# Four state-space and patch layers on one core: B rows copied ahead of the first tile's side work, and four slots for the blocks of the convolution layer

## The chip, the cores and the metric

The kernel runs on 1 core of one Trainium2 chip. The metric is the device time of one execution in microseconds. In the text PE is TensorE, ACT is ScalarE, DVE is VectorE, POOL is GpSimd and SP is SyncE, which only issues DMAs here.

## The reference, cut to what matters

x has the shape (4, 32, 32, 96): 4 images of L = 1024 positions and 96 channels. Four layers are added to it one after the other, each on the group norm of x.

```python
x = x + L0(_gn(x))    # selective scan, 4 directions, 192 channels, 16 states
x = x + L1(_gn(x))    # patches and their nearest neighbour ("motif")
x = x + L2(_gn(x))    # 3x3 convolution, then a selective scan in 1 direction
x = x + L3(_gn(x))    # as L0
```

The heart of L0, L2 and L3 is the scan over the 1024 positions, for each channel d and state n:

```python
dt = softplus(dt_proj(...) + bias)             # delta
h  = exp(dt * A[d, n]) * h + dt * u * B[n]     # along the positions
y  = sum_n h * C[n]  +  u * D
```

Behind it stand a layer norm over the channels, a product with silu(z) and an output projection.

## The kernel before

**Tiles.** A tile is 128 partitions x 1024 positions: 64 channels (a block, c = 0, 1, 2 of 192 channels) times two states. A group is the three tiles of one pair of states, which share a B row and a C row; each row is spread over 64 partitions by DMA. In L0 and L3 a turn is one image in one of two orders of its positions (row-wise, column-wise) with both directions: 2 directions x 8 pairs of states x 3 blocks = 48 tiles, t = 0 to 47, in 16 groups. There are 8 turns for each of these layers; turns 0, 2, 4 and 6 are the even ones (`r = 0`), and turns 2, 4 and 6 also finish the image before. L2 has 4 turns of 24 tiles, one for each image.

**What each tile costs.** ACT makes the decay exp(delta * A) into one of three buffers (L732, in L2 L1343). DVE makes the product of du and the B row (L872, in L2 L1480) in PSUM and then scans decay and product into one of three state buffers (L887, L1502). POOL multiplies the state by the C row into one of two read buffers (L796, L1394), and PE adds that into the y banks (L609, L1192). All of them work in program order and wait on counting semaphores.

**The B row.** `b_rows` holds one row tile. `copy_b` (L722, L1314) takes it to PSUM, where two buffers alternate by group and the spare one also holds the products of tiles c = 0 and 1. It waits for its DMA and for the scan of tile c = 1 of the group before:

```python
act.wait_ge(b_in, 32 * (G + 1))
act.wait_ge(scanned, (G - 1) * NBLK + 2 + SCAN0)
nc.scalar.copy(b_ps[g % 2][:, :], b_rows[:, :]).then_inc(b_ready, 1)
```

DVE waits for `b_ready` before the product of a group's tile c = 0. The copy stands in ACT's program ahead of decay(c=1), behind decay(c=0) and all that ACT does after that. A decay waits for the scan three tiles earlier, so decay(c=1) and the copy of a group wait for the same scan.

**Sides.** Between the tiles the engines do other work: u, bc, dt and sum of the softplus for the next turn, z, shift, cent, var and out for the image that was finished. A table gives each side product (`("dt", 2): (36, 37)` and so on, in halves) a place in PE's order of tiles, plus or minus a lag: PE computes it at tile `at` into the single PSUM bank `side_ps`, ACT takes it at tile `at + 4` (DVE cent, shift and out at `at + 3`). The next side product waits on PE until the bank is free, and the y matmuls of the tile stand behind it. The softplus has steps exp, log, one, less and relu on ACT (`ACT_SOFTPLUS`), gap and du on POOL (`POOL_SOFTPLUS`). In an even turn, ACT has at tile 36 dt2's first half and exp 1, at 37 its second half and log 1, at 38 sum 0 and one 1, at 39 sum 0's second half, less 1 and exp 2; POOL has gap 1 after read 36, and du 0 after read 37.

**SP's queue.** For each group g it issues the b row of g + 1 (`load_b`, L493, waits for copy g), then its c row (`load_c`, L504, waits for the reads of group g - 1). In L0 and L3 it also copies the blocks of delta and du of the next turn into `delta2` and `du2`, which hold every block on both halves of the partitions (L477, L478, at g = 13 and 14 of even turns, 11 and 12 of odd ones). In L2 `delta2` and `du2` have three slots, one for each block, and SP copies all three after the turn's last group, behind the c and b rows of the next turn: the copies of block q wait until the last decay and the last product of block q are done.

Of the kernel before, what the change touches and what calls it, by code (L numbers as in the profile page):

```python
# [11 lines left out]
L = H * W  # L12
# [324 lines left out]
def cross_scan_layer(nc, name, x_cm, g_cm, ident, cols_e, hbm, rank, eps):  # L337
# [4 lines left out]
    with cleared(nc) as (ctx, sems):  # L342
# [286 lines left out]
        def _(act):  # L629
# [93 lines left out]

            def turn_of(turn):
                o, number = turn.r, turn.number
                for t, (d, p, c) in enumerate(tiles):
# [198 lines left out]
def conv_scan_layer(nc, name, x_cm, g_cm, ident, hbm, rank, eps):  # L925

    NT, NJ = CONV_TILES, 2
# [5 lines left out]
    with cleared(nc) as (ctx, sems):  # L933
# [67 lines left out]
        delta2 = sb("delta2", [128, NBLK, L])  # L1001
        du2 = sb("du2", [128, NBLK, L])
# [31 lines left out]

        block = ctx.enter_context(nc.Block())
# [5 lines left out]
        def _(sp):  # L1041
# [4 lines left out]
            def copy_rows(dst, src, q, done):  # L1046

                for side in range(2):
                    if q < 2:
                        sp.dma_start(dst[quarter(side), q, :], src[0][quarter(q), :]).then_inc(done, 16)  # L1050
                    else:
                        for i, s in halves():
                            sp.dma_start(dst[quarter(side), q, s], src[1][quarter(i), :]).then_inc(done, 16)
# [42 lines left out]
            for turn in turns:  # L1096
                for g in range(NP):
# [111 lines left out]
        def _(act):  # L1209
# [120 lines left out]

            for _, key, i in head.sides:
# [3 lines left out]
            for turn in turns:  # L1335
                number = turn.number
                for t, (p, c) in enumerate(tiles):
# [5 lines left out]
                    nc.scalar.activation(decay[:, t % DECAYS, :], delta2[:, c, :], ACT.Exp,  # L1343
                                         scale=a_neg[:, c, p:p + 1]).then_inc(decay_ready, 1)
                    for at, key, i in turn.sides:
# [284 lines left out]
```

## Time and profile before

| what | value |
|---|---|
| median of 3 runs | 3991.15 us (3986.45 to 3998.62) |
| the profiled execution | 3994.56 us, its span 3992.8 us |
| granted TensorE clock, mean | 0.749 |
| PE busy | 2839.3 us, 71% |
| DVE busy | 3267.8 us, 82% |
| ACT busy | 2053.4 us, 51% |
| POOL busy | 2350.5 us, 59% |
| scans of L0 and L3 (L887) | 768, 2286 ns each |
| products of L0 and L3 (L872) | 768, 1221 ns each |
| copies of a B row (L722) | 256, 1016 ns each |

The profile is one execution. L0's turns run from 125 to 1535 us of its span, L1 until about 1760, L2's turns from 1869 to 2325, and L3's from 2505 to 3912. Times of an instruction in the rows are from the start of the span. The granted clock is that of TensorE, 1.0 being 2.4 GHz.

### The profile page before, as it was taken

To read this page: it belongs to the slowest core of one execution; us is meant where nothing else is said; L and a number is where in the kernel's file an instruction comes from. 1 tells how busy PE (TensorE), PEld (TensorE's weight loads), DVE (VectorE), ACT (ScalarE), POOL (GpSimd) and SP (SyncE) were. 2 spreads that over 40 slices of the span, in tenths; PEclk is the share of its full clock that TensorE was granted. 3 is DMA by queue.
4 is the path that set the end of the run, shared out by engine and by line. 5 is a ranking of instruction groups with operands and counts; after the bars stand their busy time and mean duration, and the time that the engine had idled before them with its cause. 6 is when DMAs were issued, how large, how long until landed. Compare 5 with 4: busy or idle time off the path is not lost. (4 is left out here: it accounts for less than half of the span.)

```text
span 3992.8 us, 26321 instructions
## 1 busy us (share of the span) xinstructions
PE 2839.3 (71%) x5888; PEld 626.3 (16%) x5888; DVE 3267.8 (82%) x2104; ACT 2053.4 (51%) x2278; POOL 2350.5 (59%) x1004
## 2 busy tenths in 40 slices
PE   3678878877877787105576664678778877887886
PEld 1111111111111111001111111111111111111111
DVE  1799999999999994373888730899999999999992
ACT  2465555656565562113455423466555656656561
POOL 0577767767676773001655521677767767776772
PEclk9767788788778775556798765677787788778885
DMA  1655556554655652002424401555636555554651
GB/s 37 138 126 133 135 124 148 130 137 113 143 133 131 142 122 54 16 4 67 105 67 105 113 14 41 135 126 132 156 102 158 129 130 122 137 135 119 156 131 32
DMA packets 140329, 436.92 MB, mean 109 GB/s; under 512 B 33383, under 2 KB 34093, under 8 KB 139869
## 3 DMA queue, kind: packets, MB, share of 16 engines
q1 hardware_dynamic: 140188, 435.53, 45.5%
q14 instruction: 112, 0.92, 0.1%
q8 instruction: 29, 0.48, 0.1%
HBM read 307.50 MB, written 6.82 MB: 79 GB/s over the span
## 5 line engine op out<-in xcount | busy, mean ns | idle before, releaser
L796 POOL TENSOR_TENSOR L_read<-L_state,L_c_rows 128x1024 f32<-128x1024 f32 x768 | 1809.4, 2363 | 754.3 <-DVE L_state L887 469.3
L887 DVE TENSOR_TENSOR_SCAN L_state<-L_decay,L_b_ps 128x1024 f32<-128x1024 f32 x768 | 1756.0, 2286 | 29.0 <-DVE L_b_ps L872 2.1
L609 PE MATMUL L_y_ps<-L_read,L_fold 128*64 128x512 f32 x3072 | 1251.0, 910 | 398.5 <-POOL L_read L796 378.3
L872 DVE TENSOR_TENSOR L_b_ps<-L_du,L_b_ps 128x1024 f32<-128x1024 f32 x768 | 937.6, 1221 | 261.6 <-issue 173.8
L732 ACT ACTIVATE L_decay<-L_delta,L_a_neg 128x1024 f32<-128x1024 f32 x768 | 876.7, 1146 | 411.2 <-DVE L_state L887 410.3
L722 ACT COPY L_b_ps<-L_b_rows 128x1024 f32<-128x1024 f32 x256 | 260.1, 1016 | 340.1 <-DVE L_state L887 217.6
L609 PEld LDWEIGHTS L_y_ps<-L_read,L_fold 128*64 128x64 f32 x3072 | 187.6, 161 | 1360.7 <-POOL L_read L796 1005.6
L1394 POOL TENSOR_TENSOR L_read<-L_state,L_c_rows 128x1024 f32<-128x1024 f32 x96 | 237.2, 2474 | 199.6 <-PE L_y_ps L1192 101.0
L589 PE MATMUL L_side_ps<-g_cm,L_w_u 96*128 (+1 forms) x216 | 189.0, 966 | 85.3 <-ACT L_u L650 45.4
L589 PE MATMUL L_side_ps<-L_dbl,L_w_dt 128*128 128x512 f32 x216 | 195.2, 1002 | 60.9 <-DVE L_sq_b L858 26.9
L1502 DVE TENSOR_TENSOR_SCAN L_state<-L_decay,L_b_ps 128x1024 f32<-128x1024 f32 x96 | 219.5, 2286 | 3.3
L1480 DVE TENSOR_TENSOR L_b_ps<-L_du,L_b_ps 128x1024 f32<-128x1024 f32 x96 | 117.3, 1222 | 95.1 <-DMA L_du<-L_du_a 75.4
L661 ACT COPY L_delta<-L_side_ps 128x512 f32<-128x512 f32 x108 | 63.1, 584 | 230.3 <-PE L_side_ps L589 230.3
L1192 PE MATMUL L_y_ps<-L_read,L_fold 128*64 128x512 f32 x384 | 125.8, 733 | 66.7 <-POOL L_read L1394 54.0
L1343 ACT ACTIVATE L_decay<-L_delta,L_a_neg 128x1024 f32<-128x1024 f32 x96 | 109.2, 1144 | 109.0 <-DMA L_delta<-L_delta_a 49.4
L1372 POOL TENSOR_TENSOR L_l_a<-L_more,L_l_a 128x1024 f32<-128x1024 f32 x4 | 9.4, 2350 | 238.1 <-ACT L_more L1272 238.1
L774 POOL TENSOR_TENSOR L_y_b<-L_more,L_y_b 128x1024 f32<-128x1024 f32 x18 | 42.6, 2365 | 168.9 <-ACT L_more L692 168.9
L589 PE MATMUL L_side_ps<-L_delta,ident 128*128 128x512 f32 x216 | 124.7, 662 | 0.0
L780 POOL TENSOR_TENSOR L_du<-L_delta,L_u 128x1024 f32<-128x1024 f32 x36 | 85.4, 2372 | 26.4 <-ACT L_delta L661 26.4
L786 POOL TENSOR_TENSOR x_cm<-x_cm,L_sq_b 96x1024 f32 (+1 forms) x8 | 18.8, 2354 | 137.2 <-DVE L_sq_b L858 137.2
L162 PE MATMUL motif_ps<-ident,motif_acc 128*96 128x128 f32 x32 | 6.4, 396 | 121.3 <-DVE motif_acc L272 121.3
L650 ACT COPY L_u<-L_side_ps 128x512 f32<-128x512 f32 x108 | 61.9, 573 | 53.9 <-PE L_side_ps L589 53.4
(301 smaller groups left out, 2718.2 us busy)
## 6 DMA issues: line engine op xcount, KB each, us to landing
L_c_rows<-L_bc_dram SPq DMA_DIRECT2D x580, 256.0 KB, 4.0
L_b_rows<-L_bc_dram SPq DMA_DIRECT2D x580, 256.0 KB, 4.1
L_delta<-L_delta SPq DMA_DIRECT2D x204, 256.0 KB, 5.6
L_du<-L_du SPq DMA_DIRECT2D x140, 256.0 KB, 5.7
L_du<-L_u SPq DMA_DIRECT2D x64, 256.0 KB, 6.0
L_bc_dram<-L_dbl SPq DMA_DIRECT2D x40, 128.0 KB, 3.4
L_delta<-L_delta_a SPq DMA_DIRECT2D x16, 256.0 KB, 6.6
L_du<-L_du_a SPq DMA_DIRECT2D x16, 256.0 KB, 7.0
```

Source lines behind the costliest of these rows:

```text
L589: m = nc.tensor.matmul(side_ps[0:rows, :], lhs, rhs, start=(k == 0), stop=(k == len(parts) - 1))
L609: m = nc.tensor.matmul(y_ps[i * BLK:(i + 1) * BLK, c, :], fold[:, :], y_half(t, o, i), start=first, stop=last, skip_group_check=True)
L722: nc.scalar.copy(b_ps[g % 2][:, :], b_rows[:, :]).then_inc(b_ready, 1)
L732: nc.scalar.activation(decay[:, t % DECAYS, :], delta2[:, d * NBLK + c, :], ACT.Exp, scale=a_neg[:, o * 2 + d, c, p:p + 1]).then_inc(decay ...
L796: nc.gpsimd.tensor_tensor(read[:, t % READS, :], state[:, t % STATES, :], c_rows[:, g % 2, :], ALU.mult).then_inc(multiplied, 1)
L872: nc.vector.tensor_tensor(to[:, :], du2[:, d * NBLK + c, :], row[:, :], ALU.mult).then_inc(injected, 1)
L887: nc.vector.tensor_tensor_scan(state[:, t % STATES, way], decay[:, t % DECAYS, way], fed[:, way], 0.0, ALU.mult, ALU.add).then_inc(scanned, 1)
L1192: m = nc.tensor.matmul(y_ps[quarter(i), c, :], fold[:, :], read[:, t % READS, s], start=t < NBLK, stop=t >= NT - NBLK, skip_group_check=True)
L1343: nc.scalar.activation(decay[:, t % DECAYS, :], delta2[:, c, :], ACT.Exp, scale=a_neg[:, c, p:p + 1]).then_inc(decay_ready, 1)
L1394: nc.gpsimd.tensor_tensor(read[:, t % READS, :], state[:, t % STATES, :], c_rows[:, p % 2, :], ALU.mult).then_inc(multiplied, 1)
L1480: nc.vector.tensor_tensor(to[:, :], du2[:, c, :], row[:, :], ALU.mult).then_inc(injected, 1)
L1502: nc.vector.tensor_tensor_scan(state[:, t % STATES, :], decay[:, t % DECAYS, :], fed[:, :], 0.0, ALU.mult, ALU.add).then_inc(scanned, 1)
```

## The change

In the three scan layers ACT's side work moves into a function `side_work(turn, t)`. It is no longer called after decay(c=0). After decay(c=1) it is called for both tiles, c = 0 and c = 1, and after decay(c=2) for that tile. The copy of a group's B row, still ahead of decay(c=1), is thereby ahead of the side work of tile c = 0. `take_y` (at tile 3) keeps its place. In L2 `delta2` and `du2` get four slots instead of three, and block q of an image lies in slot (3 * image + q) mod 4. A copy waits for the block that had the slot four blocks earlier. The copies of block 0 for the next image are issued at g = 6, after the b and c rows of the last group and ahead of the rows for the next image; blocks 1 and 2 stay at the end of the turn.

The diff, without the part that repeats it for L2's ACT program and the slot index in reads and writes:

```diff
@@ cross_scan_layer, block.scalar @@
+            def side_work(turn, t):
+
+                for at, key, i in turn.sides:
+                    if at == t - ACT_LAG and key[0] in ACT_SIDES:
+                        take(turn, key, i)
+                if turn.finish and t == SILU_AT:
+                    silu(turn)
+                if turn.finish and t == RSTD_AT:
+                    root(turn)
+                for (kind, j), at in ACT_SOFTPLUS[turn.r].items():
+                    if at == t:
+                        softplus(turn, kind, j)
+
             def turn_of(turn):
                 o, number = turn.r, turn.number
                 for t, (d, p, c) in enumerate(tiles):
...
-                    for at, key, i in turn.sides:
-                        if at == t - ACT_LAG and key[0] in ACT_SIDES:
-                            take(turn, key, i)
                     if turn.finish and t == Y_AT:
                         take_y(turn.done_image)
-                    if turn.finish and t == SILU_AT:
-                        silu(turn)
-                    if turn.finish and t == RSTD_AT:
-                        root(turn)
-                    for (kind, j), at in ACT_SOFTPLUS[o].items():
-                        if at == t:
-                            softplus(turn, kind, j)
+                    for since in ((), (t - 1, t), (t,))[c]:
+                        side_work(turn, since)
@@ conv_scan_layer @@
-    NT, NJ = CONV_TILES, 2
+    NT, NJ, SLOTS = CONV_TILES, 2, NBLK + 1
...
-        delta2 = sb("delta2", [128, NBLK, L])
-        du2 = sb("du2", [128, NBLK, L])
+        delta2 = sb("delta2", [128, SLOTS, L])
+        du2 = sb("du2", [128, SLOTS, L])
...
+        def slot(image, q):
+            return (image * NBLK + q) % SLOTS
...
             def copy_block(image, q):
 
                 sp.wait_ge(sp_du, image * NJ + q // 2 + 1)
-                if image > 0:
-                    sp.wait_ge(decay_ready, (image - 1) * NT + NT - NBLK + q + 1)
-                copy_rows(delta2, delta, q, delta2_in[q])
-                if image > 0:
-                    sp.wait_ge(injected, (image - 1) * NT + NT - NBLK + q + 1 + INJECT0)
-                copy_rows(du2, du, q, du2_in[q])
+                was, last = divmod(image * NBLK + q - SLOTS, NBLK)
+                if was >= 0:
+                    sp.wait_ge(decay_ready, was * NT + NT - NBLK + last + 1)
+                copy_rows(delta2, delta, image, q, delta2_in[q])
+                if was >= 0:
+                    sp.wait_ge(injected, was * NT + NT - NBLK + last + 1 + INJECT0)
+                copy_rows(du2, du, image, q, du2_in[q])
...
                     if g == CONV_STORE and turn.next is not None:
                         store_bc(turn)
+                    if g == NP - 2 and turn.next is not None:
+                        copy_block(turn.next, 0)
                 if turn.next is not None:
-                    for q in range(NBLK):
+                    for q in range(1, NBLK):
                         copy_block(turn.next, q)
```

## Rows read from the trace of the kernel before

**Rows 1.** the page, part 1: busy us (share of the span) xinstructions, by engine
```profile
PE 2839.3 (71%) x5888; PEld 626.3 (16%) x5888; DVE 3267.8 (82%) x2104; ACT 2053.4 (51%) x2278; POOL 2350.5 (59%) x1004
```

**Rows 2.** waits: engine, line, <- whom, us in total, times, longest
```profile
DVE L_b_ps L1480 <- DMA L_du<-L_du_a: 75.4, 8, 53.4
DVE L_b_ps L872 <- ACT L_b_ps L722: 67.3, 42, 4.6
```

**Rows 3.** timeline, DVE, L0 turn 4 (start, us, instruction, [idle <-releaser]): tiles 39, 45
```profile
973.45 1.23 DVE L872 TENSOR_TENSOR L_b_ps<-L_du,L_b_ps 128x1024 f32<-128x1024 f32 x1 [1.04 <-ACT L_b_ps L722]
...
998.83 1.23 DVE L872 TENSOR_TENSOR L_b_ps<-L_du,L_b_ps 128x1024 f32<-128x1024 f32 x1 [4.18 <-ACT L_b_ps L722]
```

**Rows 4.** timeline, ScalarE, the same turn: copy 12 to copy 15
```profile
958.39 1.02 ACT L722 COPY L_b_ps<-L_b_rows 128x1024 f32<-128x1024 f32 x1 [0.34 <-DVE L_state L887]
959.34 1.14 ACT L732 ACTIVATE L_decay<-L_delta,L_a_neg 128x1024 f32<-128x1024 f32 x1
...
966.06 0.59 ACT L661 COPY L_delta<-L_side_ps 128x512 f32<-128x512 f32 x1 [2.44 <-PE L_side_ps L589]
...
970.32 1.15 ACT L692 ACTIVATE L_more<-L_more,L_minus_col 128x1024 f32<-128x1024 f32 x1
...
997.69 1.02 ACT L722 COPY L_b_ps<-L_b_rows 128x1024 f32<-128x1024 f32 x1 [4.81 <-DMA L_b_rows<-L_bc_dram]
```

**Rows 5.** timeline, PE, the same turn: dt2's second half, sum's first
```profile
957.16 1.13 PE L589 MATMUL L_side_ps<-L_dbl,L_w_dt 128*128 128x512 f32 x2 [1.13 <-ACT L_delta L659]
...
961.69 2.07 PE L589 MATMUL L_side_ps<-L_y_a,ident 128*128 128x512 f32 x2 [2.39 <-ACT L_delta L659]
```

**Rows 6.** timeline, GpSimd, the same turn: the gap of block 1
```profile
971.61 2.36 POOL L774 TENSOR_TENSOR L_sq_b<-L_more,L_sq_b 128x1024 f32<-128x1024 f32 x1 [2.06 <-ACT L_more L692]
```

**Rows 7.** timeline, SyncE's queue, the same turn
```profile
980.96 1.08 SPq L504 DMA_DIRECT2D L_c_rows<-L_bc_dram  x2
...
990.85 2.35 SPq L493 DMA_DIRECT2D L_b_rows<-L_bc_dram  x2
```

**Rows 8.** timelines, ScalarE and DVE, L3 turn 6: less, tile 45
```profile
3699.77 1.15 ACT L692 ACTIVATE L_more<-L_more,L_minus_col 128x1024 f32<-128x1024 f32 x1
...
3728.28 1.23 DVE L872 TENSOR_TENSOR L_b_ps<-L_du,L_b_ps 128x1024 f32<-128x1024 f32 x1 [3.70 <-ACT L_b_ps L722]
```

**Rows 9.** timeline, all engines, L0 turn 4, tile 15
```profile
877.88 0.59 ACT L652 COPY L_dbl<-L_side_ps 128x512 f32<-128x512 f32 x1 [0.24 <-PE L_side_ps L589]
...
878.78 1.10 PE L589 MATMUL L_side_ps<-L_gate_a,L_w_ob_a 128*96 128x512 f32 x2
...
880.07 1.02 ACT L722 COPY L_b_ps<-L_b_rows 128x1024 f32<-128x1024 f32 x1 [1.60 <-DVE L_state L887]
...
883.40 0.66 DVE L855 TENSOR_TENSOR x_cm<-x_cm,L_side_ps 96x512 f32 x1
```

**Rows 10.** timelines, SyncE's queue and DVE, L0 turn 5, tile 39
```profile
1140.86 2.13 SPq L493 DMA_DIRECT2D L_b_rows<-L_bc_dram  x2
...
1148.66 1.23 DVE L872 TENSOR_TENSOR L_b_ps<-L_du,L_b_ps 128x1024 f32<-128x1024 f32 x1
```

**Rows 11.** timelines, L2 turn 1: PE and DVE at tile 15, DVE at tiles 21, 22
```profile
2054.04 1.07 PE L1177 MATMUL L_side_ps<-L_gate_a,L_w_ob_a 128*96 128x512 f32 x2 [1.05 <-ACT L_delta_b L1240]
...
2056.44 0.72 DVE L1462 SCALAR_TENSOR_TENSOR x_cm<-L_side_ps,L_out_bias,x_cm 96x512 f32<-96x512 f32 x1
...
2088.55 1.23 DVE L1480 TENSOR_TENSOR L_b_ps<-L_du,L_b_ps 128x1024 f32<-128x1024 f32 x1 [5.76 <-ACT L_b_ps L1314]
...
2093.10 0.68 DVE L1466 TENSOR_TENSOR L_sq_b<-L_sq_a,L_side_ps 96x512 f32<-96x512 f32 x1 [1.00 <-PE L_side_ps L1177]
```

**Rows 12.** timelines, L2, end of turn 1: GpSimd, SyncE's queue, DVE
```profile
2083.68 2.34 POOL L1377 TENSOR_TENSOR L_du_a<-L_delta_a,L_u_a 128x1024 f32<-128x1024 f32 x1
...
2096.48 1.18 SPq L1050 DMA_DIRECT2D L_delta<-L_delta_a  x2
...
2106.09 1.23 DVE L1480 TENSOR_TENSOR L_b_ps<-L_du,L_b_ps 128x1024 f32<-128x1024 f32 x1 [4.81 <-DMA L_du<-L_du_a]
```

More of the change, by code:

```diff
@@ L1044, in _, with copy_rows @@
                 sp.dma_start(to, src).then_inc(weights, 16)
-            def copy_rows(dst, src, q, done):
+            def copy_rows(dst, src, image, q, done):
                 for side in range(2):
                     if q < 2:
-                        sp.dma_start(dst[quarter(side), q, :], src[0][quarter(q), :]).then_inc(done, 16)
+                        sp.dma_start(dst[quarter(side), slot(image, q), :], src[0][quarter(q), :]).then_inc(done, 16)
                     else:
                         for i, s in halves():
-                            sp.dma_start(dst[quarter(side), q, s], src[1][quarter(i), :]).then_inc(done, 16)
+                            sp.dma_start(dst[quarter(side), slot(image, q), s], src[1][quarter(i), :]).then_inc(done, 16)
             def copy_block(image, q):
                 sp.wait_ge(sp_du, image * NJ + q // 2 + 1)
-                if image > 0:
-                    sp.wait_ge(decay_ready, (image - 1) * NT + NT - NBLK + q + 1)
-                copy_rows(delta2, delta, q, delta2_in[q])
-                if image > 0:
-                    sp.wait_ge(injected, (image - 1) * NT + NT - NBLK + q + 1 + INJECT0)
-                copy_rows(du2, du, q, du2_in[q])
+                was, last = divmod(image * NBLK + q - SLOTS, NBLK)
[5 more added lines that the diff above has]
+                copy_rows(du2, du, image, q, du2_in[q])
             def store_bc(stage):
@@ L1329, in after, with side_work @@
                     root(stage)
+            def side_work(turn, t):
+                for at, key, i in turn.sides:
+                    if at == t - ACT_LAG and key[0] in CONV_ACT_SIDES:
+                        take(turn, key, i)
+                if t == CONV_SILU_AT:
+                    silu(turn)
+                if t == CONV_RSTD_AT and turn.done is not None:
+                    root(turn)
+                if turn.next is not None:
+                    for kind, j in CONV_ACT.get(t, ()):
+                        softplus(turn, kind, j)
             for _, key, i in head.sides:
@@ L1342, in _ @@
                     act.wait_ge(scanned, number * NT + t - DECAYS + 1 + SCAN0)
-                    nc.scalar.activation(decay[:, t % DECAYS, :], delta2[:, c, :], ACT.Exp,
+                    nc.scalar.activation(decay[:, t % DECAYS, :], delta2[:, slot(number, c), :], ACT.Exp,
                                          scale=a_neg[:, c, p:p + 1]).then_inc(decay_ready, 1)
-                    for at, key, i in turn.sides:
-                        if at == t - ACT_LAG and key[0] in CONV_ACT_SIDES:
-                            take(turn, key, i)
                     if t == CONV_Y_AT and turn.done is not None:
                         take_y(turn.done)
-                    if t == CONV_SILU_AT:
-                        silu(turn)
-                    if t == CONV_RSTD_AT and turn.done is not None:
-                        root(turn)
-                    if turn.next is not None:
-                        for kind, j in CONV_ACT.get(t, ()):
-                            softplus(turn, kind, j)
+                    for since in ((), (t - 1, t), (t,))[c]:
+                        side_work(turn, since)
             take_y(B - 1)
@@ L1479, in inject_tile @@
                     dve.wait_ge(scanned, T + SCAN0)
-                nc.vector.tensor_tensor(to[:, :], du2[:, c, :], row[:, :], ALU.mult).then_inc(injected, 1)
+                nc.vector.tensor_tensor(to[:, :], du2[:, slot(number, c), :], row[:, :], ALU.mult).then_inc(injected, 1)
                 return to
```

## The prediction

> **What bounds the kernel now.** I read the page first: DVE is busy 82% of the span, more than any engine [rows 1]; in a scan layer that is one product (L872) and one scan (L887) for each tile, about 3.6 us together. What can be won is its idle time between tiles, so the second view was its waits [rows 2]: 67.3 us in 42 waits for the copy of the B row (L722) in L0 and L3, and in L2 75.4 us for the DMAs of du, 53.4 of them before the first image. The 173.8 us of "issue" are the heads of two layers, which the change leaves alone. The third view was the timeline of each engine around every such wait, since only it tells what the copy itself was waiting for.
>
> It shows two kinds. In 7 waits at tile 39 of an even turn (1.04 us in the one of [rows 3]) the copy stands behind side work of tile 39. In the eight at tile 45 (4.18 us in [rows 3], some 34 us of the 67 in all) it waits for its row: the copy comes 4.81 us after ScalarE went idle, released by a DMA [rows 4]. In 14 more, at tile 0 (0.5 to 1.7 us), it again waits for the row. A place in ScalarE's queue can't mend a late row.
>
> **Part 1: the order on ScalarE.** Instructions and durations stay (768 decays, 256 copies, the same sides). Side work of a group's first tile (c = 0) used to follow decay(c=0). Now it follows copy and decay(c=1). Both of these wait for the scan of two tiles back, one tile later than decay(c=0) had to. So this work comes up to one tile (3.6 us) plus copy plus decay (0.95 + 1.05 us from start to start, [rows 4]) later, with ScalarE idle meanwhile. Behind it stand PE's next side matmuls (one PSUM bank, freed by ScalarE) and the y matmuls behind them, GpSimd's products, SyncE's transfers. Nothing else fills the hole: before L661 at 966.06 ScalarE idles 2.44 us with later work queued [rows 4]. The Trainium skill, page PSUM — Partial Sum Buffer, section Engine vs sequencer instructions, calls ScalarE's queue strict first in, first out, which speaks against this change; by that rule, the trace agrees, held side work costs what is worked out below, and were the queue free to reorder, the part would be the pure gain of the first rival.
>
> *Even turns, tiles 36 to 45 (8 of them).* Turn 4 of L0. Before the change dt2's first half and its exp run ahead of the copy at 958.39 and free the bank for PE at 957.16 [rows 4, 5]. After the change: decay 36, idle, copy 958.4, decay 37 at 959.3, and dt2 at 960.4; the bank is free at 961.6. PE's next dt2 matmuls go from 957.16 to 961.7, ScalarE takes them at 962.8 to 964.0, PE's "sum" starts at 964.1 instead of 961.69. It now takes 4.4 us (to L661 at 966.06), its second half 2.9; so it is taken at 967.0 to 968.5. After that come "one" (1.0), decay 39 (1.1), copy 13 (1.0), decay 40 (1.1), "sum" (0.5), and "less" starts at 972.0 to 973.5, not 970.32: 1.7 to 3.2 late. I take 3.0, since PE has stood idle for some 5 us before, where after 2.39 us [rows 5] its matmuls already took twice as long. Copy 13 is at 969.5 to 971.0: the stall at tile 39 is gone.
> What does "less" release? GpSimd's gap, at 971.61 after 2.06 us of waiting [rows 6]. From there GpSimd has no pause (gap, read 37, du, read 38: four of 2.36 us) until read 38 releases the c rows at 980.96; behind them SyncE issues eight copies until 990.85, then the b row of tile 45 [rows 7], which is copied at 997.69. Tile 45 thus starts "less" + 28.5 us, whatever DVE does. L3's turn 6 bears this out: DVE has no stall at tile 39 there, and still tile 45 starts 28.51 us behind "less" (3699.77 to 3728.28, [rows 8]), to the hundredth as here (970.32 to 998.83). So 1.04 us won at tile 39 buys nothing, and 3.0 us lost at "less" arrive whole: **8 x 3.0 = +24** (13 to 26; to 37 if both sums run at the lower clock, 1.5 us more each).
>
> *Tile 15 of turns that finish an image (6 in L0 and L3).* "bc" of tile 15 is taken at 877.88, PE's shift runs from 878.78, and DVE adds it at 883.40 without waiting: 2.6 us spare [rows 9]. New: copy 880.07, decay 881.02, bc 882.1 to 882.7, shift from 882.8 to 884.8, so DVE waits 1.4 us; queued up from earlier (silu of tile 10 now starts 2.6 us late) 0.4 more. I take 1.8; at the lower clock the shift takes 3.9 and it is 3.5. **6 x 1.8 = +11** (9 to 21).
>
> *Odd turns (8).* u2 and "less" of tile 30, sum of tile 33 and sum and less of tile 36 come 2 to 4 us late. Read 32 releases c rows and eight copies, behind which the b row of tile 39 is issued at 1140.86, and DVE starts that tile at 1148.66 without a wait [rows 10]. This chain moves 1.5 to 2.7 us, against a spare of some 0.6 there and 1.3 at the next tile 0. In the four turns with stalls at 33 and 36 those go, and are mostly found again at 39. **8 x 0.7 = +6** (-4 to +12).
>
> *L2.* At tile 21 of turns 1 and 2 the copy lies behind "sum" and "var" and DVE waits 5.76 us. It will no longer. But the next thing on DVE, the out product, starts at 2093.10, released by PE at the end of the chain var, root, out [rows 11], which doesn't move: 2 x 5.76 us are only shifted 5 us on. **0** (-1 to 0). Tile 15 has the same shift as above: PE's shift starts at 2054.04, released by dt1's L1240, and DVE takes it at 2056.44 at once [rows 11]; with copy and decay first PE starts at 2056.5 and DVE at 2058.6, +2.1, and a similar 0.3 at tile 18. Turn 3 gets some 1.8 in all. **2 x 2.4 + 1.8 = +7** (0 to 12).
>
> **Part 2: four slots in L2.** At each of three image changes DVE waits for du at tiles 0 and 1: 75.4 - 53.4 = 22.0 us [rows 2], 1.3 of them in the first image. The copies can't start now before the last scans release the slots and stand behind one another on SyncE: delta from 2096.48, two issues of 1.18 us in all, then du and block 1 [rows 12]; DVE starts at 2106.09 after 4.81 us [rows 12]. With a fourth slot block 0 moves ahead of the c and b rows, right behind GpSimd's du (2083.68 + 2.34, [rows 12]), 10 us earlier, and needs no wait for a slot; its wait on SyncE holds up nothing, as the c rows behind it wait for a read until 2094. Blocks 1 and 2 take the times that blocks 0 and 1 had (four issues, 3.5 us), so block 1 lands at 2106.0, needed at 2104.9, and block 2 about when needed. Left are about 1 us there, some 3 in turn 1 for the b row (its issue comes behind the c rows and it takes about 4 to land), and 0.5 to 1 more for the copy of tile 3, which stays behind take_y. That is 5.1 each: **-15.4** (-8 to -21, nearly all of it). [...]
>
> **Sum.** +24 + 11 + 6 + 0 + 7 - 15.4 = +32.6. The profiled execution took 3994.6 us (span 3992.8), 3.4 over the median 3991.15; changes carry over, so 3991.15 + 32.6 = **4024 us**.
>
> **Rivals.**
> 1. *The waits on the copy were the loss, as counted* (PE and GpSimd absorb the later sides). Gone: 67.3 less 34 (tile 45) and 15 (tile 0) = 18, 11.5 at tile 21, 15.4: -45, 3946 us. For it: the waits name the copy [rows 3]. Against: the 28.51 us that hold with and without a stall at tile 39 [rows 3, 8], and out in L2. It decides if "less" starts no later than now. 10%.
> 2. *Only the slots count*: the sides come late but within spare time everywhere (the tile-15 slack of 2.6 us suffices, sum runs at full clock behind an early dt2). -15, 3976 us. 12%.
> 3. *The lower clock joins in*: idle PE falls to 1.2 GHz and both sums and the shift take the long time: 37 + 21 + 12 + 9 - 12 = +67, 4058 us. 10%.
> Forecast, with its own range 4000 to 4045: 68%.
>
> A measurement here tells 0.3% (12 us) from no change. Slower, above 4003: 64 of the forecast's 68 and rival 3, 74%. Same: its other 4 and 6 of rival 2, whose 3976 lies near the bound, 10%. Faster: rival 1 and the rest of rival 2, 16%. The range leaves out rival 1, a third of rival 2 and half of rival 3, 19%: 3970 to 4057.
>
> **What would show it.** DVE's waits on L722 lose those at tiles 33, 36 and 39 of the old places, but those at 45 grow from 4.3 to 8 or are partly turned into waits for GpSimd (scan 41 needs read 38, now at 984); new waits of the shift add (L855 in L0 and L3, L1462 in L2) for PE, 1.5 to 3.5 us; in L2 5.8 us more before L1466; du waits at image changes down from 21 to 2 to 7. Wrong would be: "less" of an even turn at its old place, no waits at L855, or tile 45 early although "less" is late.

## The result, and the profile after

| | before | after |
|---|---|---|
| median of 6 runs beside each other | 3990.68 us (3981.49 to 3998.62) | 4065.03 us (4062.0 to 4082.8) |
| span of the profiled execution | 3992.8 us | 4061.4 us |
| granted TensorE clock, mean | 0.749 | 0.735 |

The ratio is 1.0194, with an interval of 1.0172 to 1.0217: 74 us slower, where the prediction had 33 and a range that ended at 4057. The direction was right and the size was not.

The page of after, part 1, and its list of DVE's waits (us in total, times, longest), which answer to [rows 1] and [rows 2]:

```profile
PE 2868.5 (71%) x5888; PEld 635.9 (16%) x5888; DVE 3264.4 (80%) x2104; ACT 2045.5 (50%) x2278; POOL 2345.3 (58%) x1004
```

```profile
DVE x_cm L860 <- PE L_side_ps L589: 79.9, 10, 24.4
DVE L_b_ps L877 <- ACT L_b_ps L722: 76.2, 36, 5.2
DVE L_b_ps L1496 <- DMA L_du<-L_du_a: 54.7, 2, 53.4
DVE x_cm L1478 <- PE L_side_ps L1188: 45.4, 7, 20.9
...
DVE L_state L892 <- POOL L_read L801: 41.9, 35, 2.6
```

The reader is to see that no engine has more work: the instructions are as many as before, DVE's busy time is 3 us less and its share falls from 82 to 80%. Only PE is busy longer, 29 us, with the same 5888 matmuls at a lower mean clock. The waits grew. Those on the copy are 76.2 us, not 67.3, so the change makes longer what it was to remove. The shift add (L860, L855 before) waits 79.9 us in 10 places, 57.7 us in 5 before. The scans wait 41.9 us for GpSimd's reads, 0.8 before. Only du's DMAs in L2 went down, from 75.4 to 54.7 us.

The starts of the products in the timelines of both kernels give the length of each stretch of a turn, and so the place of the loss. Sums over all such turns, us, after against before:

| stretch | predicted | measured |
|---|---|---|
| finishing turns, tiles 0 to 15 (6) | +11 | +23.4 |
| even turns, tile 33 to the end (8) | +24 | +26.7 |
| odd turns (8) | +6 | +21.8 |
| L2, up to L3's first product | -8.4 | -0.3 |
| the rest (-3.9 of it ahead of L0's first product) | 0 | -3.0 |
| sum | +32.6 | +68.6 |

The term of the even turns is near what was reckoned, those of tile 15 and of the odd turns are far too small, and what L2 was to win did not come. The sum is that of the two profiled executions; the medians are 74.4 us apart.

These lengths scatter from one execution to another. In `slots_only`, `order_l2`, `held_6`, `held_9_15`, `held_15` and `held_15_fill` below, the even turns behind tile 33 and the odd turns are those of before, and yet their sums differ from before's by -9.9 to +2.1 us (even) and by -4.4 to +2.7 (odd). Before's own trace is thus on the long side in even turns: against the other traces the change costs some 31 us there, the mean, and not 26.7.

### The profile page after: what moved, and what is told of

It is laid out like the page before. It is cut to its first block and busy times, and to the rows that moved or that the text cites. A ratio compares the mean times of both kernels' runs of the same rounds, so it can differ in the third digit from the quotient of the medians.

```text
span 4061.4 us, 26320 instructions
## 1 busy us (share of the span) xinstructions
PE 2868.5 (71%) x5888; PEld 635.9 (16%) x5888; DVE 3264.4 (80%) x2104; ACT 2045.5 (50%) x2278; POOL 2345.3 (58%) x1004
## 5 line engine op out<-in xcount | busy, mean ns | idle before, releaser
L892 DVE TENSOR_TENSOR_SCAN L_state<-L_decay,L_b_ps 128x1024 f32<-128x1024 f32 x768 | 1755.8, 2286 | 69.3 <-POOL L_read L801 41.9
L609 PE MATMUL L_y_ps<-L_read,L_fold 128*64 128x512 f32 x3072 | 1268.0, 925 | 361.6 <-POOL L_read L801 343.2
L1496 DVE TENSOR_TENSOR L_b_ps<-L_du,L_b_ps 128x1024 f32<-128x1024 f32 x96 | 117.3, 1222 | 71.5 <-DMA L_du<-L_du_a 54.7
L1203 PE MATMUL L_y_ps<-L_read,L_fold 128*64 128x512 f32 x384 | 131.5, 765 | 52.5 <-POOL L_read L1410 45.4
L589 PE MATMUL L_side_ps<-L_delta,ident 128*128 128x512 f32 x216 | 116.3, 621 | 0.0
L589 PEld LDWEIGHTS L_side_ps<-L_dbl,L_w_dt 128*128 128x128 f32 x216 | 47.9, 276 | 287.6 <-ACT L_delta L659 165.5
```

The costliest lines, as they stand in the source:

```text
L589: m = nc.tensor.matmul(side_ps[0:rows, :], lhs, rhs, start=(k == 0), stop=(k == len(parts) - 1))
L609: m = nc.tensor.matmul(y_ps[i * BLK:(i + 1) * BLK, c, :], fold[:, :], y_half(t, o, i), start=first, stop=last, skip_group_check=True)
L892: nc.vector.tensor_tensor_scan(state[:, t % STATES, way], decay[:, t % DECAYS, way], fed[:, way], 0.0, ALU.mult, ALU.add).then_inc(scanned, 1)
L1203: m = nc.tensor.matmul(y_ps[quarter(i), c, :], fold[:, :], read[:, t % READS, s], start=t < NBLK, stop=t >= NT - NBLK, skip_group_check=True)
L1496: nc.vector.tensor_tensor(to[:, :], du2[:, slot(number, c), :], row[:, :], ALU.mult).then_inc(injected, 1)
```

## Experiments

All are the kernel before with parts of the change, unless it says otherwise. Times stand against the runs of before made beside them.

**The change in its parts.** `slots_only` has part 2 alone, `order_l2` and `order_l0` have the new order on ScalarE in L2 alone or in L0 and L3 alone. The edits are those of the diff above, layer by layer. `copy_only` moves the copy in L0 and L3 ahead of the side work, but leaves decay(c=1) behind it:

```diff
                     if c == 1:
                         copy_b(number * GROUPS + p + NP * d, (p + NP * d))
+                        side_work(turn, t - 1)
...
-                    for since in ((), (t - 1, t), (t,))[c]:
-                        side_work(turn, since)
+                    if c > 0:
+                        side_work(turn, t)
```

> Before with part 2 alone: four slots in L2, block 0 copied at g = 6, ScalarE's old order in all layers. The traces of before and after show L2 as a whole at -0.3 us. Theory: the slots win what was reckoned for them, and the new order in L2 gives it back: -8 to -15 us, so 3976 to 3983, and the product's waits for du (L1480 in before) fall from 22 to under 7 us outside the first image. Rival: the waits for du only turn into waits for the B row and the copy at the same place, and nothing is won: 3988 to 3994.

> Before with the new order on ScalarE in L2 alone, three slots. Theory (the counterpart of the one for the slots): +7 to +15 us, 3998 to 4006, from new waits of the shift add at tile 15 and 18 (4 us each in the trace of after) and from the out product. Rival: L2's order change is neutral, the stall of 5.76 us at tile 21 pays for the two shift waits: 3988 to 3994.

> Before with the new order in L0 and L3 alone, nothing changed in L2. From the lengths of the turns in the two traces: finishing turns up to tile 33 +24, even turns behind it +27, odd turns +22, heads -4, together +69: 4055 to 4065. Rival: the slots or L2 have a share in the loss (through the granted clock, which fell from 0.749 to 0.735): 4030 to 4050.

> Before with the copy alone moved, in L0 and L3: decay(c=0), copy, side work of tile c = 0, decay(c=1), side work of c = 1. The copy waits for the same scan as decay(c=1), so the side work is still held for it, but by a decay (1.05 us) less, and the side work of two tiles is parted by a decay. Theory: the wait for the scan in front of the side work is what costs; 60 to 90% of the loss of the kernel with the new order in L0 and L3, +42 to +62, 4033 to 4053. Rival: it is the decay put in front and the two tiles' work in one piece that cost, as two halves of a side product must pass one bank: under a third of the loss, 3991 to 4013.

| kernel | median, us | against before | ratio, interval |
|---|---|---|---|
| slots_only | 3970.03 | -19.9 | 0.9954 (0.9940 to 0.9967) |
| order_l2 | 4006.62 | +16.7 | 1.0040 (1.0026 to 1.0054) |
| order_l0 | 4066.78 | +76.8 | 1.0190 (1.0173 to 1.0207) |
| copy_only | 4027.63 | +37.7 | 1.0093 (1.0077 to 1.0108) |

The three parts add up to +73.6, and the whole change has +74.4, so each can be judged by itself. The order in L0 and L3 is most of the miss (+76.8 where 24 + 11 + 6 = 41 was reckoned, 36 of the 42 us). The slots give somewhat more than I expected here, and in L2 the order costs more than the 7 of the prediction. `copy_only` came out at half of `order_l0`, below my 60 to 90% and above the rival's third, so both matter: that side work waits for the copy's scan, and that decay(c=1) stands ahead of it as well. By stretches, the copy alone costs 1.8 us up to tile 15 of the finishing turns, where the whole order costs 23.1, then 11.9 for 29.7 in even turns and 14.4 for 20.6 in odd ones.

**Which group holds what.** In the next kernels the new order holds for single groups of tiles only. `held_6` has group 2 of the finishing turns, `held_9_15` their groups 3 to 5, `held_15` group 5. `held_a`, `held_b` and `held_c` have one group in each of three stretches. The edit of `held_b`, set against the new order:

```diff
-                    for since in ((), (t - 1, t), (t,))[c]:
+                    late = t // NBLK in (10,) if o else t // NBLK in (4, 12,)
+                    for since in (((), (t - 1, t), (t,))[c] if late else (t,)):
                         side_work(turn, since)
```

> Before, with the new order on ScalarE in the six finishing turns of L0 and L3 for group 2 alone (tiles 6 to 8), old order everywhere else. The kernel with the new order throughout L0 and L3 loses 23.1 us between tiles 0 and 15 of these turns. In the windows, PE is busy 13.7 to 14.1 of 14.1 us in tiles 4 to 7 of before, at a clock of 0.95 to 0.98. Theory: this is the stage with no slack; z's halves held at tile 6 make a backlog on PE that reaches the shift at tile 15, six times 2 to 4: +12 to +23, 4002 to 4013, with new waits of the shift add (L860 here) at tile 15. Rival, the prediction's own account: only what is held at tile 15 counts, and a hold at tile 6 is made good before it: 3987 to 3994.

> Before, with the new order in the six finishing turns for groups 3 to 5 alone (tiles 9 to 17: u, silu, bc). The prediction's account: 6 x 1.8 = +11 (9 to 21), 3999 to 4012. Theory of the backlog from tiles 4 to 8: here the turn gets to tile 9 without one, so the wait at tile 15 is 0.5 to 1.8 us, +3 to +11, 3993 to 4001; the two together leave the 23.1 us of the whole to both.

> Before with the new order on ScalarE in L0 and L3 for single groups only: group 3 (tiles 9 to 11: u0, silu) and group 11 of even turns, group 9 (tiles 27 to 29) of odd ones. Read by stretches of a turn. The prediction's account: 0.4 us at most at tile 15, nothing in odd turns, even turns nothing at tile 33. Rival (a hold works through groups before): 1 us or more at tile 15, 1 us or more in odd turns between tiles 27 and 39.

> The same for group 4 (tiles 12 to 14: u1, bc) and group 12 of even turns (tiles 36 to 38: dt2, exp, sum), group 10 of odd ones (tiles 30 to 32: u2, less, sum). The prediction's account: nothing at tile 15, most of the 3.0 us behind tile 39 in even turns, under 1 us in odd turns. Rival: 1 to 3 us at tile 15 through u1, and 2 to 3 us in odd turns, as less at tile 30 holds GpSimd's gap and with it all reads up to the c row.

> The same for group 5 (tiles 15 to 17: bc) and group 13 of even turns (tiles 39 to 41: sum, less, exp), group 11 of odd ones (tiles 33 to 35). The prediction's account: 1.4 us at tile 15, some 1 us behind tile 39 in even turns (less behind decay 40), -1.4 in those odd turns that have a stall at tile 33. Rival: nothing at tile 15 when the groups before it are on time (2.6 us spare), the loss of 3.7 us there needs groups 3 to 5 together.

`held_6` took 3986.55 us, ratio 0.9993 (0.9983 to 1.0003): nothing. My theory of the backlog from tile 6 fell, and the prediction's account held there. `held_9_15` took 4011.47 us, +22.4, ratio 1.0060 (1.0046 to 1.0075). Growth by stretches in the traces (sums over the turns, us; the last three kernels ran once each, at 3992.96, 4054.53 and 4028.99 us):

| kernel | finishing, 0 to 15 | even, 33 to end | odd, whole |
|---|---|---|---|
| order_l0 | +23.1 | +29.7 | +20.6 |
| held_9_15 | +20.1 | | |
| held_a (groups 3; 11; 9) | +3.6 | -7.8 | +2.8 |
| held_b (groups 4; 12; 10) | +17.5 | +20.0 | +20.5 |
| held_c (groups 5; 13; 11) | +17.4 | +10.8 | +3.7 |

In even turns groups 12 and 13 together make 30.8, the whole order 29.7, in the proportion that the prediction gave them; with the scatter above, this sum can be off by several us. In odd turns group 10 alone makes all of it. Up to tile 15, group 4 alone or group 5 alone costs nearly as much as groups 3 to 5 together (group 5 some 3.3 us in five turns, group 4 1 us in two turns and 3.2 to 5.2 in four). The four are just those in which the granted clock was 0.53 to 0.54 in tiles 4 to 7, ahead of the held group; in the other two it was 0.98 and 0.75. What group 4 costs by itself is thus the 1 us, and the rest goes with the clock. The -7.8 of `held_a` lies within the scatter. "less" of tile 39 has two places there, 19.1 to 20.5 us or 17.6 us behind the start of tile 33. The later one came in seven even turns of before and in two of `held_a`. What decides between them is not shown.

ScalarE's timeline shows the hold of group 10, in turn 5 of L0 of `held_b`:

```profile
1126.69 1.15 ACT L745 ACTIVATE L_decay<-L_delta,L_a_neg 128x1024 f32<-128x1024 f32 x1 [0.85 <-DVE L_state L893]
1130.27 1.02 ACT L722 COPY L_b_ps<-L_b_rows 128x1024 f32<-128x1024 f32 x1 [2.43 <-DVE L_state L893]
1131.22 1.15 ACT L745 ACTIVATE L_decay<-L_delta,L_a_neg 128x1024 f32<-128x1024 f32 x1
1132.27 0.56 ACT L650 COPY L_u<-L_side_ps 128x512 f32<-128x512 f32 x1
```

and the same place of before, whose turn began at 1010.52, not at 1027.43:

```profile
1109.79 1.15 ACT L732 ACTIVATE L_decay<-L_delta,L_a_neg 128x1024 f32<-128x1024 f32 x1 [0.85 <-DVE L_state L887]
1110.84 0.57 ACT L650 COPY L_u<-L_side_ps 128x512 f32<-128x512 f32 x1
...
1113.37 1.02 ACT L722 COPY L_b_ps<-L_b_rows 128x1024 f32<-128x1024 f32 x1 [0.91 <-DVE L_state L887]
```

u2's first half is taken 104.84 us after the turn's start, 100.32 before: 4.5 us later, and 2.43 of them ScalarE stands idle with this work ready. It is the full price of a hold: the wait for the scan, the copy (0.95) and the decay (1.05). SyncE's issue of tile 39's row, 130.34 us after the turn's start before [rows 10], comes at 134.53 here:

```profile
1161.96 2.16 SPq L493 DMA_DIRECT2D L_b_rows<-L_bc_dram  x2
```

So 4.2 of the 4.5 us come through, not 1.5 to 2.7.

**The shift at tile 15.** One question was left here. With group 5 held, bc's second half is taken 51.8 us after the turn's start, as the prediction had it (882.1 less 830.3). Still DVE waits 3.2 us, not 1.4. `held_15` has group 5 of the finishing turns alone, and `held_15_fill` adds two matmuls with weights of zero in the hole on PE, so PE idles less ahead of the shift (the lines that set up `zero_w` are left out):

```diff
+                    if turn.finish and t == 12:
+                        for _ in range(2):
+                            nc.tensor.matmul(y_ps[0:BLK, 0, :], zero_w[0:C, :], g_half(turn.next_image, 0, 0),
+                                             start=False, stop=False, skip_group_check=True)
                     for at, key, i in turn.sides:
                         if at == t:
                             side(turn, key, i)
```

> Before with the new order on ScalarE in L0 and L3 for group 5 alone (tiles 15 to 17) of the finishing turns. In the kernel that also had other groups in other stretches, tiles 0 to 15 of these turns grew by 3.4 us each (one 1.0), and PE stood idle for 2.0 us ahead of the shift. Expected: the same here, 17 to 23 us in all, 4003 to 4012.

> The same, and on PE two matmuls of the shift's length with weights of zero ahead of the shift's first half in these turns (they add zero to y), in the 2 us in which PE otherwise waits for bc. Theory: it is the lower granted clock after the idle time that makes the shift take 4.1 us instead of 2.0; with the hole filled the shift runs at 2.4 GHz and the wait at tile 15 falls from 3.4 to 1.0 to 1.8 us: 10 to 14 us under the kernel without the filling. Rival: the clock has nothing to do with it, or the filling itself stands in the way: the wait stays at 3.4 us or grows, same time or slower.

Timeline of PE at the shift of tile 15, L0 turn 4, and under it what the shift add waited (DVE), `held_15`:

```profile
883.57 1.88 PE L589 MATMUL L_side_ps<-L_gate_a,L_w_ob_a 128*96 128x512 f32 x2 [3.81 <-ACT L_dbl L652]
885.38 2.02 PE L589 MATMUL L_side_ps<-L_gate_b,L_w_ob_b 64*96 64x512 f32 x2
...
887.57 0.68 DVE L861 TENSOR_TENSOR x_cm<-x_cm,L_side_ps 96x512 f32 x1 [3.21 <-PE L_side_ps L589]
```

and `held_15_fill`:

```profile
884.11 1.88 PE L604 MATMUL L_y_ps<-g_cm,L_zero_w 96*64 x4
887.69 1.10 PE L590 MATMUL L_side_ps<-L_gate_a,L_w_ob_a 128*96 128x512 f32 x2 [1.69 <-ACT L_dbl L657]
888.72 1.09 PE L590 MATMUL L_side_ps<-L_gate_b,L_w_ob_b 64*96 64x512 f32 x2
...
889.98 0.68 DVE L867 TENSOR_TENSOR x_cm<-x_cm,L_side_ps 96x512 f32 x1 [1.50 <-PE L_side_ps L590]
```

The windows over these two shifts (us; busy time of PE, its weight loads, DVE, ACT and POOL; granted clock; DMA share; GB/s), `held_15` and then `held_15_fill`:

```profile
883.50:887.40 3.90, 3.83 (x6) 0.72 (x8) 0.86 (x1) 1.17 (x2) 0.00 (x0) 0.53 0.41 130
```

```profile
887.60:889.90 2.30, 2.21 (x6) 0.64 (x8) 0.88 (x1) 1.18 (x2) 0.00 (x0) 1.00 0.73 200
```

After 3.81 us of idleness the shift's matmuls run at 1.2 GHz, and the shift add starts 4.0 us behind the first of them. After 1.69 us they run at 2.4 GHz and it starts 2.3 us behind, and DVE waits 1.50 us, what the prediction had reckoned for the full clock. The filling does it in three of the six turns, whose tiles 0 to 15 then grow by 1.61 us each (in two of them only 0.3 us of idleness was left); in turns 2 and 6 of L0 and turn 6 of L3 the clock fell in spite of it, after 1.84, 2.08 and 1.84 us, and the first two grow by 2.8 and 3.3. In the sum of the six it is 11.6 us, where `held_15` has 17.2. The length of the hole alone does not decide it: in three turns of `held_15` it is only 1.7 to 1.8 us, and the shift runs at 1.2 GHz all the same. The Trainium skill, page TensorE: Matmul & The Clock Gate, section Part 1: The HAM clock gate (the "warmup" mystery), calls the low clock the default state that activity releases; by that rule, the trace agrees, at 0.53 behind the long hole and 1.00 behind the short one. Over the whole kernel the 10 to 14 us that were expected did not come, and the filling is worth less than a run can tell: 4012.35 and 4006.98 us, ratios 1.0057 (1.0042 to 1.0072) and 1.0037 (1.0024 to 1.0050), whose intervals overlap.

This is what the shift does where group 5 alone is held. In the change itself it is otherwise, as the next section shows. L2 does have the same at its tile 15. PE's timeline in turn 1 of after; before, the matmuls took 1.07 us after 1.05 of idleness [rows 11]:

```profile
2084.23 1.99 PE L1188 MATMUL L_side_ps<-L_gate_a,L_w_ob_a 128*96 128x512 f32 x2 [3.60 <-ACT L_delta_b L1251]
```

**The late row.** `spread` has the four slots, the old order, and the copies of block 1 for the next turn one group later; `thirds` has blocks 0, 1 and 2 at g = 13, 14 and 15 in even turns, `thirds_all` also 11, 12 and 13 in odd ones. `order_spread` and `order_thirds` have these lists with the new order in L0 and L3 (three slots). `thirds`:

```diff
-COPY_BELOW, COPY_ABOVE = (1, 2, 3), ((13, 13, 14), (11, 11, 12))
+COPY_BELOW, COPY_ABOVE = (1, 2, 3), ((13, 14, 15), (11, 11, 12))
```

> The kernel with the four slots alone, and with the copies of block 1 for the next turn one group later on SyncE (g = 14 in place of 13 in even turns, 12 in place of 11 in odd ones), so that four copies, not eight, stand ahead of the B row of tile 45 (39). The prediction's account: tile 45 waits because the row is late behind these copies. Theory: the waits on the copy at tile 45 (4.2 us, 8 times) fall by 2.5 to 4.2 each, and nothing else takes their place before the turn's end: -20 to -34 against the four slots alone, 3936 to 3950. Rival: GpSimd's reads are as late as the row, and the wait only changes its name: 3965 to 3972.

> The new order in L0 and L3 (three slots in L2, old order there) and the copies of block 1 one group later on SyncE, as in the kernel beside it. With the order alone the loss behind tile 33 is 54 us, and 23 us before tile 15. Theory: in odd turns (27 us per kernel) and in even ones the held side work reaches DVE through GpSimd's read, the c row, the copies and the B row; with four copies in the way the row has some 5 us of slack, which takes up the 3 us of the hold, and GpSimd's reads are left: 30 to 50 us under the kernel with the order alone, 4017 to 4037. Rival: the held work reaches DVE through GpSimd's reads alone, and the row is not needed for it: 4055 to 4067.

> The kernel with the four slots alone, and in even turns the copies of blocks 0, 1 and 2 for the next turn at g = 13, 14 and 15 (13, 13, 14 before), odd turns as before. In the kernel with blocks 1 and 2 both at g = 14 the wait at tile 45 was gone, and the same 4.2 us stood at tile 0 of the next turn, whose rows came behind eight copies. Theory: four copies ahead of each row fit; tile 45 and tile 0 keep a wait of 1.1 us at most, block 2 lands about when tile 2 needs it, up to 2 us late: -18 to -34 against the four slots alone, 3936 to 3952. Rival: decay(t=2) waits for block 2 and ScalarE with it, so that copy and sides behind it are late and all is given back: 3965 to 3975.

> Four slots, old order, and the copies of blocks 0, 1 and 2 one group after another in both kinds of turns (g = 13, 14, 15 in even, 11, 12, 13 in odd ones; the kernel with it in even turns alone took 3964). In odd turns the wait at tile 39 is 0.4 us in some of them and 1.1 at tile 0. Theory: four copies ahead of each row fit there too: 0 to -6 against that kernel, 3958 to 3964. Rival: as in the kernel with two blocks at g = 12, the row of tile 42 is late behind the copies, +2 a turn: 3970 to 3985.

> The new order in L0 and L3 with the copies of blocks 0, 1 and 2 at g = 13, 14 and 15 in even turns (old order and three slots in L2). In the kernel with the order alone, tiles 39 to the end of an even turn lose 4.3 us each. The prediction's account is that the held side work arrives through the row of tile 45, behind eight copies. By it, with four copies in the way the row has some 5 us of slack, and even turns lose at most 1 to 2 us behind tile 39: 18 to 30 us under the kernel with the order alone, 4037 to 4049. Rival: GpSimd's reads of tiles 36 to 42 are as late as the row, and carry the hold by themselves: 0 to 10 us under it, 4057 to 4067.

| kernel | median, us | against before | ratio, interval |
|---|---|---|---|
| spread | 3996.21 | +7.1 | 1.0017 (1.0005 to 1.0028) |
| order_spread | 4090.53 | +101.4 | 1.0254 (1.0241 to 1.0267) |
| thirds | 3964.03 | -23.9 | 0.9941 (0.9929 to 0.9954) |
| thirds_all | 3967.90 | -23.8 | 0.9940 (0.9926 to 0.9954) |
| order_thirds | 4061.76 | +70.0 | 1.0182 (1.0168 to 1.0196) |

`spread` and `order_spread` came out slower than theory and rival had it, each of them. DVE's timeline from tile 45 of turn 4 to tile 0 of turn 5, `spread`:

```profile
1000.91 2.29 DVE L887 TENSOR_TENSOR_SCAN L_state<-L_decay,L_b_ps 128x1024 f32<-128x1024 f32 x1 [0.43 <-POOL L_read L796]
1015.62 1.23 DVE L872 TENSOR_TENSOR L_b_ps<-L_du,L_b_ps 128x1024 f32<-128x1024 f32 x1 [5.39 <-ACT L_b_ps L722]
```

Tile 45 no longer waits 4.18 us [rows 3]; that part of the mechanism is shown. But tile 0 of the next turn waits 5.39 us, not 1.11: the eight copies now stand ahead of its rows. In odd turns, with eight copies ahead of the row of tile 42, that tile waits 2.27 us in turn 5 and 2.1 to 4.0 in all eight; before has none there. Against `slots_only` the traces have +19.1 us in odd turns, +1.7 behind tile 33 of even ones, and +7.8 up to tile 15 of finishing turns, four of which have the low clock told of below. `thirds` leaves 3.26 us at tile 0, and tile 45 free: 0.9 us less an even turn than in `slots_only`. It is the fastest version here, 24 us under before, though its interval and that of `slots_only` (-19.9) overlap. The -18 to -34 that were expected against `slots_only` did not come, since tile 0 waits three times what I allowed it. `thirds_all` adds nothing to it.

`order_thirds` brings tile 39 to the end of even turns from 34.8 us of loss to 24.3, half of what I expected from the row, and 5 us in the total, where the rival had 0 to 10. DVE's timeline in turn 4:

```profile
994.93 2.29 DVE L892 TENSOR_TENSOR_SCAN L_state<-L_decay,L_b_ps 128x1024 f32<-128x1024 f32 x1 [1.89 <-POOL L_read L801]
999.56 2.29 DVE L892 TENSOR_TENSOR_SCAN L_state<-L_decay,L_b_ps 128x1024 f32<-128x1024 f32 x1 [1.22 <-POOL L_read L801]
1013.17 1.23 DVE L877 TENSOR_TENSOR L_b_ps<-L_du,L_b_ps 128x1024 f32<-128x1024 f32 x1 [0.71 <-ACT L_b_ps L722]
...
1028.70 1.23 DVE L877 TENSOR_TENSOR L_b_ps<-L_du,L_b_ps 128x1024 f32<-128x1024 f32 x1 [4.34 <-ACT L_b_ps L722]
```

The row of tile 45 costs 0.71 us and the loss stands elsewhere: in scans that wait for GpSimd's reads, and in the row of the next tile 0, which SyncE issues behind the c row that waits for those reads. The right comparison is with `thirds`, which has the same copies and the old order: behind tile 33 of even turns it has -12.5 us, `order_thirds` +19.3, so the order costs 31.8 with these copies and 29.7 with the old ones. "less" comes 3.5 us later in `order_thirds` than in `thirds`, and tile 45 stands 24.3 us behind it in the one and 24.4 in the other (means of the eight turns). So the hold arrives whole through GpSimd's reads, and the late row isn't needed for it. The rival was right. What the row adds is a wait of its own, 28.7 us from "less" to tile 45 in place of 24.4, and `thirds` has 2.6 of these 4.3 us again up to the next tile 0.

## Why the prediction was wrong in size

**The even turns were right in mechanism.** The prediction said that "less" would come 3.0 us late and tile 45 28.5 us behind it, whatever DVE does. ScalarE and DVE in after, L0 turn 4, which answer to [rows 3, 4]:

```profile
990.06 1.15 ACT L692 ACTIVATE L_more<-L_more,L_minus_col 128x1024 f32<-128x1024 f32 x1
```

```profile
996.17 2.29 DVE L892 TENSOR_TENSOR_SCAN L_state<-L_decay,L_b_ps 128x1024 f32<-128x1024 f32 x1 [2.62 <-POOL L_read L801]
1000.81 2.29 DVE L892 TENSOR_TENSOR_SCAN L_state<-L_decay,L_b_ps 128x1024 f32<-128x1024 f32 x1 [1.23 <-POOL L_read L801]
1018.75 1.23 DVE L877 TENSOR_TENSOR L_b_ps<-L_du,L_b_ps 128x1024 f32<-128x1024 f32 x1 [5.04 <-ACT L_b_ps L722]
```

1018.75 less 990.06 is 28.69 us. "less" stands 149.92 us behind the turn's start, 140.03 before; without the 5.7 us lost up to tile 15 it is 4.2 late. That is over the 3.0 I took in this turn. In the mean of the eight "less" is 3.4 us late, and tile 45 starts 28.4 to 28.9 us behind it in every one, before as after; the stretch has +26.7 for +24. The wait at tile 45 grew from 4.18 to 5.04 us, and two scans wait 3.85 us for reads, as was said.

**The term for tile 15 failed.** The prediction had "bc 882.1 to 882.7, shift from 882.8 to 884.8", a wait of 1.4 us, and for what is queued up from earlier "0.4 more". The step that failed is this 0.4: it takes bc as ready where it was before, and holds it once, at tile 15. PE, ScalarE and DVE in after, L0 turn 4, which started at 840.14:

```profile
885.45 2.08 PE L589 MATMUL L_side_ps<-g_cm,L_w_u 96*128 x2 [6.56 <-ACT L_u L650]
...
889.36 2.04 PE L589 MATMUL L_side_ps<-L_u,L_w_bc_a 128*128 128x512 f32 x2
...
896.01 0.57 ACT L652 COPY L_dbl<-L_side_ps 128x512 f32<-128x512 f32 x1
896.63 1.10 PE L589 MATMUL L_side_ps<-L_gate_a,L_w_ob_a 128*96 128x512 f32 x2
...
898.93 0.68 DVE L860 TENSOR_TENSOR x_cm<-x_cm,L_side_ps 96x512 f32 x1 [4.38 <-PE L_side_ps L589]
```

and the window over this shift:

```profile
896.00:899.00 3.00, 2.94 (x10) 0.68 (x8) 0.07 (x1) 1.63 (x3) 2.27 (x1) 1.00 0.73 175
```

PE waited 6.56 us for ScalarE to take the first half of u, side work of group 4. bc's product comes after that, and bc's second half is taken 55.87 us behind the turn's start, not 51.8. The shift then runs at the full clock, as before (1.10 us for the pair). It is so in all six finishing turns of after: bc's second half is taken at 52.8 to 55.9 us, the shift takes 2.1 us, and the add waits 2.5 to 4.7 us. That is within 0.2 us the 1.4 of the prediction and the lateness of bc, but for turns 4 and 6 of L0, which had lost 1.1 and 0.3 us of it at tile 12. `order_l0` and `held_9_15` show the same. So the shift at 1.2 GHz, which the prediction named as its other end (3.5 us) and which `held_15` has in all six turns, is not what happened here. That 3.5 is near the mean wait of 3.8 us in after is luck: holding group 5 alone costs 17.2 us by a slow shift, and holding groups 3 to 5 costs 20.1 by a late bc and a fast shift.

The lower clock does take part, but ahead of bc. Behind that hole a pair of bc's matmuls takes 2.04 us, 1.13 before. How much of bc's lateness is hold and how much is clock, no run separates. A second part stands earlier still. The windows of tiles 4 to 7 of turn 4 in L0, before and then after:

```profile
844.60:858.70 14.10, 13.72 (x40) 2.57 (x36) 13.86 (x9) 7.15 (x8) 9.43 (x4) 0.98 0.90 207
```

```profile
854.50:868.60 14.10, 14.10 (x30) 2.63 (x28) 13.89 (x9) 6.38 (x7) 5.89 (x3) 0.54 0.68 149
```

At 2.4 GHz PE is busy for 13.7 of 14.1 us there; at 0.54 it can't follow, and GpSimd's busy time falls from 9.4 to 5.9. In the finishing turns of before the clock is 0.95 to 0.98 in this window in five turns, and 0.55 in turn 6 of L3. After has it at 0.54 to 0.55 in three; these grow by 5.0 to 5.7 us up to tile 15, the other three by 1.4 to 3.4 (the 1.4 is turn 6 of L3, which was 2.0 longer than its like before). Before and the five other kernels that leave tiles 0 to 15 of these turns as they were (`slots_only`, `order_l2`, `spread`, `thirds`, `thirds_all`) have 36 of them. Five have 0.55 to 0.57 in this window and are 1.7 to 2.1 us longer than their like; the others (0.74 to 0.98) agree within 0.1 us. So the low clock goes with the longer turns; under the new order this is less strict (turn 4 of L3 in `order_l0` had 0.55 and grew by 3.4 us, like its neighbours at 0.74 to 0.76). Why it falls is not shown: four of the five stand in `spread`, with the old order, and `held_b` had it in four turns, in a stretch whose order is that of before.

**The term for odd turns failed.** The step was "this chain moves 1.5 to 2.7 us, against a spare of some 0.6". The chain moves 4.2 us (group 10 of `held_b`), since side work of the group's first tile waits for the scan and then for copy and decay, 4.5 us in all. The prediction gave such a hold as up to 5.6 us where it described the new order, and didn't use that here. In turn 5 of after, tile 39 starts 3.6 us later in its turn than before, 2.30 of them as a wait for the copy. Such a wait stands at tile 39 of all eight odd turns of after, 19.6 us in all, where before had 2.9 in four of them. By the prediction's signs the waits at tile 39 were to go.

**L2.** The slots gave -14.6 us between L2's first and last product (-15.4 predicted), and in the timed runs -19.9, within the bound of 21. The order cost +16.7 for +7, with an interval of 10 to 22 that reaches to the upper bound of 12. In its trace L2 is 17.8 us longer from first to last product, but L3's first product follows 7.3 us sooner, as DVE waits less for the last image's side products behind the tiles: +10.5. Of this, 3.4 stand in turn 0, for which the prediction had nothing. In after the two parts give -0.3 us together; at the first image change DVE waits 7.02 us for the copy there, 4.05 in `slots_only`. At tile 15 of turns 1 and 2 the shift add waits 4.02 and 4.12 us for its two halves, where it waited for the second alone, 2.28 us: +5.9 a turn where 2.4 was reckoned. Here it is the low clock on the shift, after 3.60 us of idleness. That the stall of 5.76 at tile 21 is only shifted was right: out now waits 6.03 us, where the two together had 6.76.

**The rivals.** Rival 3, the lower clock joining in (4058 us, 10%), comes nearest in the number, and the measured 4065 lies behind it, but its path holds only in part: the shift took the long time in L2 and not in L0 and L3, and the odd turns' +12 in it were 21.8. Rivals 1 and 2 are out: "less" came later than before, and the order cost 77 us by itself. As for the signs to look for: waits at L855 of 1.5 to 3.5 us came as 2.5 to 4.7, the waits for du of blocks 0 and 1 at image changes are gone, those of block 2 are 0.6 to 0.9 us, and tile 0 waits 7.02, 1.10 and 0.76 us for the copy and its row; tile 45 has 5.04 us and the two scans ahead of it 3.85, together over the 8 foretold.

## What to carry to other kernels

An engine in program order that is made to wait earlier holds all that comes after it: price the hold as the full wait plus everything put ahead, follow it through every queue, and test the spare time against that sum. Where groups are held one after the other, add up the holds: the second acts on work that the first has made late. Where a hold leaves TensorE idle, reckon its next matmuls at the lower clock as well, and find out which matmuls those are. A transfer that is late behind others is not mended by moving those behind it, if they then stand ahead of the next row.

## What was not expected of the hardware

- Holes of nearly the same length gave two clocks for the same matmuls. After 1.69 us of idleness the shift ran at 2.4 GHz (1.10 us for each pair), after 1.84 and 2.08 us the clock fell to 1.2 GHz during it or at its start (1.35, then 2.02; 1.84, then 2.02), as after 3.81 us (1.88, then 2.02). In three turns of `held_15` it ran at 1.2 GHz from its first matmul, after 1.7 to 1.8 us.
- A stretch in which PE is busy 97% at 2.4 GHz has two courses that differ by some 2 us, at a clock of 0.74 to 0.98 or of 0.55 to 0.57, in the same code: the slower came in before once in six turns (turn 6 of L3), in `spread` four times, and in `held_6` once with +2.0 us.
- Work of one place in a turn came at two times in the same code: "less" of tile 39, 17.6 us or 19.1 to 20.0 us behind tile 33, in before once and seven times.
